# Two layer-0 groups taken tile by tile in turn, and LoRA spread over 16 steps, in a two-layer gated cross-attention kernel

## What is computed

```
x = x + tanh(g_xattn[0]) * L0_xattn(layernorm(x), ctx)   # 32 heads of 128, 8 kv heads, q and k rms-normalized
x = x + tanh(g_ffn[0])   * L0_lora(layernorm(x))         # low = x A^T; router softmax over 8; out = sum of score * low * B
x = x + tanh(g_xattn[1]) * L1_xattn(layernorm(x), ctx)   # 16 heads of 96, 4 kv heads
x = x + tanh(g_ffn[1])   * L1_ffn(layernorm(x))          # silu(gate) * up, down, inner width 1792
```

## Time and profile before

| | |
|---|---|
| median of 3 runs | 1186.69 us (1186.66 to 1187.54) |
| profiled execution | 1187.59 us, span 1185.8 us |
| PE busy | 1126.9 us (95%), granted clock 0.989 of 2.4 GHz |
| DVE busy | 854.2 us (72%) |
| ACT busy | 825.2 us (70%) |
| POOL busy | 371.1 us (31%) |
| DMA | 139.56 MB, mean 118 GB/s |
| chain that ended last | PE 80%, DVE 10%, ACT 3%, issue 3%, POOL 2%, DMA 1% |

### The profile page before, as it was taken

How to read it: one execution, slowest core, us unless ns; L and a number is a source line. 1 busy time by engine, 2 the same in 40 slices (tenths; PEclk the granted TensorE clock), 3 DMA queues, 4 the chain that set the end, 5 groups by cost and what they waited for, 6 DMA issues and landing times.

```text
span 1185.8 us, 22717 instructions
## 1 busy us (share of the span) xinstructions
PE 1126.9 (95%) x7184; PEld 710.5 (60%) x7184; DVE 854.2 (72%) x2066; ACT 825.2 (70%) x2695; POOL 371.1 (31%) x669
## 2 busy tenths in 40 slices
PE   6689999999999999999999998799999999799998
PEld 4445666666666666666666655566766766455554
DVE  5577767767767667777677789998888888743434
ACT  5678888888888888878888766677787765522221
POOL 5454434334733333333343454322111121000000
PEclk8899999999999999999999999999999999999999
DMA  7366654463655545555445746668996786200000
GB/s 246 101 126 138 130 125 101 119 143 85 139 147 120 116 109 126 129 104 131 119 99 116 143 98 134 136 140 171 232 189 144 136 173 122 49 1 1 36 1 36
DMA packets 411992, 139.56 MB, mean 118 GB/s; under 512 B 386656, under 2 KB 396640, under 8 KB 411872
## 3 DMA queue, kind: packets, MB, share of 16 engines
q1 hardware_dynamic: 409968, 134.43, 51.7%
q0 software_dynamic: 1904, 3.67, 1.1%
HBM read 39.21 MB, written 2.10 MB: 35 GB/s over the span
## 4 chain that ended last, share of the span: by engine, by line
PE 80%; DVE 10%; ACT 3%; issue 3%; POOL 2%; DMA 1%; DVEq 0%; POOLq 0%; ACTq 0%
PE bank L518 23%; PE bank L519 22%; PE bank L520 22%; PE bank L719 8%; PE bank L738 4%; DVE pieces L1079 1%; DVE mx L1182 1%; ACT probs L901 1%; DVE stats L1090 1%; DVE x L1219 1%; ACT junk L810 1%; DVE lg L1237 1%; DVE xn L1102 1%; POOL rstd L1474 1%; DVE q_rows L1079 1%
## 5 line engine op out<-in xcount | busy, mean ns | idle before, releaser
L807 ACT ACTIVATE pieces<-probs,rs 128x256 f16<-128x256 f32 x384 | 166.0, 523 | 10.4 <-DVE rs L1199 9.0
L1182 DVE TENSOR_REDUCE mx<-bank 128x2 f32<-128x512 f32 x192 | 131.5, 685 | 55.6 <-PE bank L520 55.4
L901 ACT ACTIVATE probs<-bank,nb,rq 128x256 f32<-128x256 f32 x256 | 141.1, 563 | 41.1 <-DVE nb L1187 40.6
L1079 DVE SCALAR_TENSOR_TENSOR pieces<-probs,rs,pieces 128x256 f16<-128x256 f32 x384 | 163.2, 485 | 5.6 <-ACT pieces L807 4.8
L518 PE MATMUL bank<-wq,xT 128*128 128x512 f16 (+1 forms) x384 | 139.5, 363 | 2.7 <-DVE wq L1079 2.7
L810 ACT ACTIVATE junk<-bank 128x128 bf16<-128x128 f32 x384 | 101.6, 287 | 55.2 <-PE bank L520 55.2
L518 PE MATMUL bank<-wo_hi,oT 128*128 128x512 f16 x352 | 134.0, 381 | 5.7 <-DVE oT L1079 4.3
L519 PE MATMUL bank<-wq,xT 128*128 128x512 f16 (+1 forms) x384 | 139.4, 363 | 0.0
L520 PE MATMUL bank<-wq,xT 128*128 128x512 f16 (+1 forms) x384 | 139.2, 363 | 0.0
L519 PE MATMUL bank<-wo_lo,oT 128*128 128x512 f16 x352 | 134.2, 381 | 0.0
L520 PE MATMUL bank<-wo_hi,oT 128*128 128x512 f16 x352 | 134.1, 381 | 0.0
(11 more groups left out here) (185 smaller groups left out, 2638.7 us busy)
## 6 DMA issues: line engine op xcount, KB each, us to landing
raw_o<-in_wo_a SPq DMA_DIRECT2D x8, 1024.0 KB, 6.0
raw_q<-in_wq_a SPq DMA_DIRECT2D x7, 1024.0 KB, 6.0
raw_kv<-in_wkv_a SPq DMA_DIRECT2D x8, 512.0 KB, 3.8
turned<-pieces SPq DMA_TRANSPOSE x192, 2.8
raw_q<-in_wq_c SPq DMA_DIRECT2D x4, 768.0 KB, 5.1
raw_o<-in_wo_c SPq DMA_DIRECT2D x4, 768.0 KB, 4.9
down_rest<-in_down_t POOLq DMA_DIRECT2D x5, 512.0 KB, 4.2
ff_in<-in_gate_t SPq DMA_DIRECT2D x4, 448.0 KB, 4.2
```

What stands on the lines that cost most here:

```text
L807: return act.activation(out, in_, ACT.Copy, scale=scale)
L901: act.activation(probs[:, h, :], bank[h // 2][:, (h % 2) * KV:(h % 2 + 1) * KV], ACT.Exp, bias=nb[:, h:h + 1], scale=scale, accum_out=sums ...
L1079: return dve.scalar_tensor_tensor(out, in_, scale, hi, ALU.mult, ALU.subtract)
L1182: dve.tensor_reduce(mx[:, pr], chunks(bank[i][:, :], 2), AX.X, ALU.max, negate=True).then_inc(mx_done, 1)
```

## The change

Layer 0's last two groups alternate: pair n = 48 + 2t is group 6's tile t, 49 + 2t is group 7's tile t (`place`). Norm 1 of tile t is in step 51+2t, LoRA in 52+2t, norm 2 in 53+2t. As both groups are in use together, there is a third set of weights for group 6, in the memory of the context staging buffer (`set_of_group`: groups 0 to 5 use g % 2, group 6 set 2, groups 7 to 11 (g+1) % 2), and the weights of groups 4 to 7 are made in fewer and earlier steps (`making`: load, square, scale, chunks). LoRA's output goes to bank 3. `nb` is a `tensor_tensor` in layer 0 and a `tensor_scalar` in layer 1. ScalarE's high piece of norm 2 comes ahead of that of norm 1. Scales per group have three slots instead of two.

```
+def place(n):
+    first = N0 - 2 * NT
+    if first <= n < N0:
+        return L0.groups - 2 + (n - first) % 2, (n - first) // 2
+    return divmod(n, NT)
...
-    return (tile(n + 4) if n + 4 >= 4 and n < 4 else None, tile(n - N0 + 6), tile(n - N0 + 5), tile(n - N0 + 4),
-            tile(n - (N - NT) - 3))
+    def second(m):
+        return tile(m // 2) if m % 2 == 0 else None
+
+    first = N0 - 2 * NT + 3
+    return (tile(n + 4) if n + 4 >= 4 and n < 4 else None, second(n - first), second(n - first - 1),
+            second(n - first - 2), tile(n - (N - NT) - 3))
...
+def set_of_group(g):
+    if g < L0.groups - 2:
+        return g % 2
+    return 2 if g == L0.groups - 2 else (g + 1) % 2
...
+def making(kind, g):
+    b = g * NT
+    special = {
+        ("kv", 1): (None, 0, 1, (1, 2)), ("q", 1): (None, 1, 2, (2, 3, 4, 4)), ("o", 1): (1, 3, 4, (4, 5, 6, 7)),
+        ("q", 4): (21, 23, 24, (25, 25, 26, 26)), ("o", 4): (24, 26, 27, (28, 28, 29, 30)),
+        ("q", 5): (27, 29, 30, (31, 32, 32, 33)), ("o", 5): (31, 33, 34, (35, 36, 36, 37)),
+        ("kv", 6): (32, 34, 35, (36, 37)), ("q", 6): (34, 36, 37, (38, 38, 39, 39)),
+        ("o", 6): (38, 40, 41, (42, 42, 43, 43)),
+        ("kv", 7): (38, 41, 42, (43, 44)), ("q", 7): (40, 42, 43, (44, 44, 45, 45)),
+        ("o", 7): (44, 46, 47, (48, 48, 49, 49)),
+    }
+    if (kind, g) in special:
+        return special[kind, g]
+    if kind == "kv":
+        return b - 14, b - 12, b - 11, (b - 10, b - 9)
+    if kind == "q":
+        return b - 11, b - 9, b - 8, (b - 7, b - 6, b - 5, b - 4)
+    return b - 8, b - 6, b - 5, (b - 4, b - 3, b - 2, b - 1)[:layer_of_group(g).oc]
...
+        w2 = nc.alloc_sbuf_tensor_at("w2", [P, 10 * KC * 2 * P], F16, offset=stage_at)
...
             def square_kv(g):
                 act.wait_ge(in_kv, 16 * (g + 1))
-                if g >= 2:
-                    act.wait_ge(kv_done, NT * (g - 1))
+                if owner_before(g) is not None:
+                    act.wait_ge(kv_done, last_step(owner_before(g)) + 1)
+                if set_of_group(g) == 2:
+                    act.wait_ge(lw_done, 3)
...
             def lora_project_out(t):
                 pe.wait_ge(lora_lo, t + 1)
-                mm3(bank[2][:, :], tT[t % 2], lb, start=True, stop=True).then_inc(lora_out, 1)
+                if t >= 1:
+                    pe.wait_ge(lora_added, t)
+                mm3(bank[3][:, :], tT[t % 2], lb, start=True, stop=True).then_inc(lora_out, 1)
...
-                if lora is not None and lora >= 1:
-                    pe.wait_ge(lora_added, lora)
-                if n == N0 + 3:
-                    pe.wait_ge(lora_added, NT)
...
+                if norm2 is not None:
+                    norm_row_hi(2, norm2)
                 if norm1 is not None:
                     norm_row_hi(1, norm1)
                 if lora is not None:
                     router_exp(lora)
-                if norm2 is not None:
-                    norm_row_hi(2, norm2)
...
-                    dve.wait_ge(yadd_done, N0 - NT + t + 1)
+                    dve.wait_ge(yadd_done, N0 - 2 * NT + 2 * t + 2)
...
-                    dve.scalar_tensor_tensor(nb[:, pr], mx[:, pr], 1.0, rq[:, c:c + 2], ALU.mult, ALU.mult
-                                             ).then_inc(nb_done, 1)
+                    dve.tensor_tensor(nb[:, pr], mx[:, pr], rq[:, c:c + 2], ALU.mult).then_inc(nb_done, 1)
...
-                    dve.scalar_tensor_tensor(nb[:, pr], mx[:, pr], es[:, g % 2, s:s + 1], zeros[:, :], ALU.mult, ALU.add
-                                             ).then_inc(nb_done, 1)
+                    dve.tensor_scalar(nb[:, pr], mx[:, pr], es[:, g % 3, s:s + 1], None, ALU.mult).then_inc(nb_done, 1)
```

More of the change, by code:

```diff
@@ L149, in build @@
         cT = tuple(chunks(w, KC) for w in pair("cT", KC * TOK))
[L150 to L156, removed]
+        wq0 = sb("wq0", 2 * KC * NH * P, F16)
+        wq1 = sb_at("wq1", 2 * KC * NH * P, F16)
+        wkv0 = sb("wkv0", 2 * KC * 2 * P, F16)
+        wkv1 = sb_at("wkv1", 2 * KC * 2 * P, F16)
+        wo0, wo1 = sb("wo0", 2 * NH * D, F16), sb("wo1", 2 * NH * D, F16)
         raw_q_all = sb_at("raw_q", KC * NH * P)
@@ L336, in group_pair, with in_step @@
         def group_pair(s, g):
-            return s[:, 2 * (g % 2):2 * (g % 2) + 2]
+            return s[:, 2 * (g % 3):2 * (g % 3) + 2]
         def lora_part(w, j):
             return chunks(w, KC)[:, :, 0:P] if j == 0 else chunks(w, KC)[:, :, P:LW]
[L344 to L368, removed]
+        def in_step(kind, stage, n):
+            found = [g for g in range(1, GROUPS) if making(kind, g)[stage] == n]
+            return found[0] if found else None
         def weight_chunks(n):
@@ L373, in weight_chunks @@
                 return [("o", 0, j) for j in range(4)]
[L374 to L383, removed]
+            return [(kind, g, j) for kind in ("kv", "q", "o") for g in range(1, GROUPS)
+                    for j, at in enumerate(making(kind, g)[3]) if at == n]
         ctx.enter_context(nc.allow_low_precision(reason="sums of squares that only choose a scale"))
@@ L462, in step @@
                     turn(S, 1)
[L463 to L469, removed]
+                for kind, load in (("kv", load_kv), ("q", load_q), ("o", load_o)):
+                    g = in_step(kind, 0, n)
+                    if g is not None:
+                        load(g)
                 if 70 <= n < 70 + 2 * KC:
@@ L562, in kv_proj @@
                     for k in range(KC):
-                        done = mm3(out, tile_of((cT, xT)[i], k, t), cols(wkv[g % 2], kv_cols(g, k)), start=k == 0,
+                        done = mm3(out, tile_of((cT, xT)[i], k, t), cols(wkv[set_of_group(g)], kv_cols(g, k)), start=k == 0,
                                    stop=k == KC - 1)
@@ L568, in q_proj @@
             def q_proj(n):
-                L, g, t = layer_of(n), n // NT, n % NT
+                L, (g, t) = layer_of(n), place(n)
                 if n >= 2:
@@ L581, in q_proj @@
                         pe.wait_ge(wq_done, KC * g + k + 1)
-                    last = mm3(q_bank(n)[:, 0:L.qw], tile_of(xT, k, t), cols(wq[g % 2], q_cols(g, k)), start=k == 0,
+                    last = mm3(q_bank(n)[:, 0:L.qw], tile_of(xT, k, t), cols(wq[set_of_group(g)], q_cols(g, k)), start=k == 0,
                                stop=k == KC - 1)
@@ L845, in square_q @@
                     act.wait_ge(in_q, 16 * (g + 1))
-                if g >= 2:
-                    act.wait_ge(q_done, NT * (g - 1))
-                squares(wq[g % 2][1][:, sl], raw_q[:, sl], ssq[:, 2 + half:3 + half]).then_inc(ssq_q, 1)
+                if owner_before(g) is not None:
+                    act.wait_ge(q_done, last_step(owner_before(g)) + 1)
+                squares(wq[set_of_group(g)][1][:, sl], raw_q[:, sl], ssq[:, 2 + half:3 + half]).then_inc(ssq_q, 1)
             def square_o(g, half):
@@ L852, in square_o @@
                 act.wait_ge(in_o, 16 * (g + 1))
-                if g >= 2:
-                    act.wait_ge(y_done, NT * (g - 1))
-                squares(wo[g % 2][1][:, sl], raw_o[:, sl], ssq[:, 4 + half:5 + half]).then_inc(ssq_o, 1)
+                if owner_before(g) is not None:
+                    act.wait_ge(y_done, last_step(owner_before(g)) + 1)
+                squares(wo[set_of_group(g)][1][:, sl], raw_o[:, sl], ssq[:, 4 + half:5 + half]).then_inc(ssq_o, 1)
             def square_lora():
@@ L1514, in q_norm @@
             def q_norm(n):
-                g = n // NT
+                g = place(n)[0]
                 c = slice(NH * (n % 2), NH * (n % 2) + NH)
@@ L1561, in o_scale @@
                     pool.wait_ge(iu_tanh_done, 2)
-                pool.tensor_scalar(ty[:, g % 2, :], iu_tanh[:, 0 if g < L0.groups else 1, :],
+                pool.tensor_scalar(ty[:, g % 3, :], iu_tanh[:, 0 if g < L0.groups else 1, :],
                                    group_pair(s_v, g)[:, 1:2], group_pair(s_o, g)[:, 1:2], ALU.mult, ALU.mult
@@ L1631, in step @@
                     k_norm(T)
-                for scaled, scale in ((kv_scaled, kv_scale), (q_scaled, q_scale), (o_scaled, o_scale)):
-                    if scaled(n) is not None:
-                        scale(scaled(n))
+                for kind, scale in (("kv", kv_scale), ("q", q_scale), ("o", o_scale)):
+                    g = in_step(kind, 2, n)
+                    if g is not None:
+                        scale(g)
                 if n == 21:
@@ L1671, in _ @@
             norm_rstd(0, 1)
[L1672 removed]
+            pool.wait_ge(consts, 8)
             kv_scale(0)
```

89 lines of the change are left out of this document (47 added, 42 removed).

## The result

The changed kernel takes 1177.11 us (median of 4 runs, 1175.12 to 1177.39), the kernel before 1187.12 (4 runs); the ratio is 0.991, with a 95% interval of 0.9893 to 0.9927. The forecast was 1174.0, a gain of 12.7 us, with a range of 1166 to 1182; 10.0 us were gained. The profiled execution took 1177.13 us with a span of 1175.3.

What follows compares the result with a forecast made beforehand. VectorE's in-order queue was taken to set steps 59 to 68, TensorE the plain steps. 20.0 us gained there less 7.3 lost in steps 51 to 58 gave -12.7, from a median of 1186.69 to 1174.0; range 1166 to 1182.

Steps and rivals of the forecast that it cites:

- The chains: VectorE's time from o_low's start to y_add's: layer 0 even 8.8, odd 9.7; layer 1's tiles odd 8.4, even 7.7 us.
- Tails: VectorE's time from y_add to the next o_low: 3.2 us in even steps, 0.67 in odd ones.
- The sum: Chains, tails and chunks of steps 59 to 68: 102.9 instead of 122.88 us, 20.0 gained; 7.3 lost in steps 51 to 58.
- Tie and lag: Layer 0 pairs cost VectorE and TensorE 22.4 us each; VectorE's allowed lag, about 3 us in plain steps, hides work.
- about 91 us: Time predicted for steps 51 to 58 after the change, instead of 83.6 us.
- Bank 3 counted at nothing: Removing lora_project's waits for lora_add, 2.5 + 0.8 us, is already inside the sum and not counted again.
- Weights at nothing, bounds 0 and +5: Making weights of groups 4 to 7 in fewer steps costs 0; upper bound about 0.2 us in each of 25 steps.
- `nb`, memset and order at nothing: New nb forms, one memset less and norm 2's high piece first: 0; GpSimd at most 0.6 us later.
- Smooth hand-over: Rival: the lag covers everything, TensorE never waits; -21.8, 1164.9 us; chance 0.15. Steps 62 and 65 spoke against it.
- The stall moves along: Rival: LoRA steps still take their present time, odd steps what their columns need; -5.4, 1181.3 us; chance 0.15.
- three signs: Wrong if layer 0 pairs exceed 24 us, kn holds back kv_proj, or TensorE waits during the weights' early making.
- Slower: Rival: early weights in steps 25 to 49 make everything behind a late load late; 1191 us; chance 0.08.

Runs made afterwards that it cites:

- 2: The changed kernel with groups 6 and 7 alternating but norm 1, LoRA and norm 2 one tile a step in steps 58 to 67: 1190.0 us.
- 8: The changed kernel with one more statistics instruction on VectorE in each of steps 59 to 66: 1179.9 us (one run).
- 7: The changed kernel with one more statistics instruction on VectorE in each of steps 51 to 58: 1181.5 us (one run).
- 11: The changed kernel with one matmul a block instead of three for LoRA's projection of tiles 0 to 3, computation left out: 1174.6 us (one run).
- 9: The changed kernel with norm 1's high piece first and group 8's kv and q chunks made in steps 49 to 51: 1173.6 us.
- 3: The changed kernel with LoRA's output in bank 2 again, TensorE waiting for lora_add: 1176.5 us.
- 5: The changed kernel with norm 1's high piece ahead of norm 2's again on ScalarE: 1174.8 us.
- 4: The kernel before with only the new nb forms, no memset of zeros, and norm 2's high piece ahead of norm 1's: 1188.9 us, ratio 1.0008.

## Why the prediction was right, and where its sum was off

*What bounds the kernel.* Right: the gain lies in the steps where VectorE's queue set the time. Experiments 2 and 8 show it.

*The chains.* Even steps of layer 0: 8.8 predicted, 8.51 to 9.00 measured (steps 54 to 60). Odd ones: 9.7, measured 9.55 to 9.92. Layer 1's tiles: odd 8.4, measured 8.53 and 8.15; even 7.7, measured 7.34, 7.56 and 8.03. Tails: 3.2 and 0.67, measured 3.19 and 0.66. From `o_low` of step 59 to that of step 69, 684.65 to 787.58, it is 102.93 us; the sum had 102.9. That it agrees to 0.03 is luck: step 62 was 0.4 shorter than its term (11.72 against 12.1) and step 66 0.3 longer (10.83 against 10.5), and such errors cancel.

*The sum.* Then why are steps 59 to 68 18.1 us shorter and not 20.0? I added periods from `o_low` to `o_low` and set them against 122.88, which runs from `y_add` to `y_add`. With LoRA only behind step 58 the two agreed within 0.3 (122.62 from `o_low` 677.47 to 800.09). Now step 58 holds tile 3, and its tail of 3.71 us lies behind the first cut, while step 68's of 1.85 lies behind the last. That is the 1.9 us. The loss in front of it is 6.6 instead of 7.3, and the net 11.5 instead of 12.7. Cut at `o_low` throughout, it is 19.7 gained in steps 59 to 68 and 8.0 lost in steps 51 to 58 (84.36 before, 92.31 now). Either way what the sum lacks is the tail of step 58, 1.6 us longer than before (3.71 against 2.11): it lay in neither of its two terms. (The 0.4245 ns a column are the mean of 0.4251 in layer 0's plain steps and 0.4239 in layer 1's, which changes nothing here.)

*Tie and lag in steps 51 to 58.* The tie is right (7, 11, 9), and "about 91 us" were 90.20.

*Bank 3 counted at nothing.* Right (2, 3).

*Weights at nothing, bounds 0 and +5.* Right: no wait of TensorE in steps 25 to 49, pairs 0 to 49 +0.1.

*`nb`, memset and order at nothing.* Wrong: the order alone costs 2.0 us in the changed kernel (5), and the three edits together 1.5 in the dense one (4). "At most 0.6 us later for GpSimd" was 1.1 us: ScalarE's first copy now waits 0.98 us for norm 2's `xn`, which VectorE makes second, instead of 0.36. The two 128x2 forms are no cheaper than the old (0.16 as before; 0.228 against 0.221). The one-input form was held for 1.04 us. That agrees with the lock of the Trainium skill (SBUF — State Buffer, "SBUF: two separate sides") if this form runs in a two-port mode, which no trace tells. And a row did show it ahead: L1237 in the earlier trace rows, held for 1.016 us, is a `tensor_scalar` with one tensor as input too, and the prediction overlooked it.

*Rivals and signs.* "Smooth hand-over" fails: TensorE waits 7.1 us in the listing, 1.28 at once in step 62 and 2.06 behind step 65, the two steps named against it. "The stall moves along" is right in one point: `kv_proj` waits for `kn`, 2.6 us, and VectorE for `kr`; not in size. With it came one of the three signs that I had named for being wrong, `kn` holding back `kv_proj`. The periods of VectorE came out as summed all the same, each of steps 62 to 66 within 0.4, so the sign alone said nothing on the size. The layer 0 pairs stayed at 24 us or less (steps 59 and 60, with three chunks, 24.00). "Slower" has no trace in steps 25 to 49.

*The rest.* -1.1 at the start and +2.0 in pairs 66 to 79 lie in no step that the sum changed. The kernel of experiment 4, which is the kernel before but for `nb` and order, has 79.15 for pairs 70 to 79 against 77.43, the changed kernel without low pieces 77.59; profiles of that stretch differ by as much without a cause that I know. Whether `nb`'s form has any part in it stays open.

## What to carry to other kernels

Where one engine's queue is the bound in some steps and another's in their neighbours, moving work over gains what the first queue gets shorter, less what the neighbours can't take in their own time. Add up chains and tails step by step, and check that the sum and the measured stretch have the same cuts. A wait listed at TensorE names what was late there, not a price: here those for `lora_add` were removed without any gain, as the next wait took their place. And an engine that is busy for 99% of a stretch need not be its only bound: here work added to VectorE and work taken from TensorE told the tie.

## What the runs showed of the hardware

- GpSimd's two subtractions run back to back for 2.27 us, but a held VectorE instruction waits for one at most: 1.09 us, it gets in between them. This was so for two inputs (L1208) and for one (L1212, 1.04).
- The first `y_add` moved between 77.24 and 79.64 us over the twelve profiles of kernels with the new buffers, which do the same work before it. Between before and changed, where it is 1.1 us, TensorE's waits for ScalarE's piece of `wo` (4.3 against 2.7 us) and for `xn` (1.6 against 0.7) in the first 50 us differ; I followed it no further.
- In pairs 70 to 79 the DMA engines are busy for 91 to 97% of the time, and these pairs take 77.4 to 80.9 us over the profiles, with TensorE waiting, nearly always before `values`, for 0.8 to 3.7 us.
